# Moving the router products of the second stage from the head of a tile to behind the transposes of its activated rows

## The chip, the cores and the metric

The kernel runs on one NeuronCore of a Trainium2 chip. The metric is the device time of one execution in microseconds. Three runs of the kernel before are given, and one further execution was recorded by the hardware profiler; every duration used below is from that one.

## The reference, cut to what matters

The reference is one decoder layer over 2048 tokens (4 sequences of 512) with rows of 512 numbers. It has three blocks, each followed by a residual sum and a layer norm:

```python
x = _layernorm(x + attn(x, ...))       # 16 heads, chunked linear attention, gated group norm
x = _layernorm(x + xattn(x, token_ids, ctx, ctx, ctx))   # 4 experts, chosen by token id
x = _layernorm(x + ffn(x, gate_weight, gate_up, down))   # 48 kept experts, top 8 by a router
```

The second block is, for the one expert e to which a token belongs, with the same 512 by 512 matrix W three times:

```python
s = x @ W[e].T
y = (silu(s) * s) @ W[e]
```

The third block begins with a router, whose logits are taken from the rows that the second block has just normed:

```python
logits = x @ gate_weight.T              # 48 of the 128 columns are kept
top_v, top_i = top_k(softmax(logits), 8)
```

## The kernel before, in words

The kernel has three stages: attention (tiles of 128 tokens), the second block (called the second stage here), and the 48 experts with the closing norm. Each engine has its own list of instructions, written out by hand, and the engines meet through semaphores alone. An instruction that waits holds up everything behind it on its engine.

The second stage works on 19 tiles of 128 slots (`SLOT_T`), sorted by expert so that a tile has one expert. Every engine walks the tiles with `slot_tiles`, which calls its `b_tile(j, p, k, left, place)`: tiles 0 to 4 are written out, tiles 5 to 16 are a loop of three turns with four tiles in its body, and tiles 17 and 18 are written out again. Here j is the tile, p = j % 2 and k = j // 2; `is_later(j)` is true from tile 2 on.

Three tiles are in hand at once. TensorE's `b_tile(j)` (L898) issues, in this order:

- `route(p, k - 1)` (L890, matmuls at L895): the router's logits of tile j-2, four products of a 128x128 block of normed rows with 48 columns, which the profile shows as eight matmuls. It waits for ScalarE's copy of the transposed rows (`x2T_copied`) and ends in `lg_made`.
- `turn_h(p, k, 0)` (L875, L879): two transposes of the first half of `h1`, the activated rows of tile j. It waits for `h1_made`, which VectorE's `hidden` raises for each half (L1635).
- `expert_of(j)` (L853): TensorE's sequencer reads the number of tile j's expert from memory into a register (`value_load`).
- `turn_x` (L859, L863): four transposes of the gathered rows of tile j+1.
- `turn_h(p, k, 1)` (L879): two transposes of the second half of `h1`. It ends in `h1_turned`, on which ScalarE copies all of it, rounded, into `o_hi` (L1267).
- `turn_x2` (L883, L887): four transposes of the normed rows of tile j-1, for which it waits on `x2_made`.
- the down product of tile j: 12 matmuls at L629 of 512 columns (issued from L910), which wait for `o_high`, and from the ninth on for `h1_copied`.
- `up` of tile j+1: 24 matmuls at L629 of 256 columns. Each half raises `s_made`; ScalarE makes silu of it (L1253), VectorE multiplies (`hidden`, L1635) and raises `h1_made`.

VectorE's `b_tile(j)` has, in this order: `route(p, k - 1)` (L1637), which waits for `lg_made` of tile j-2 and is a chain of small instructions (L1642 to L1649); `low_h` (L1653), the rest of the activated rows that `o_hi` leaves over; `low_x1` (L1658), the same of tile j+1's gathered rows; `route_weights` (L1682 to L1699) of tile j-2; the residual sum of tile j at L1713, which waits for the down product (`y1_made`); its statistics (L1715, L1718); both halves of `hidden` of tile j+1 (L1635); and the norm of tile j (L1727), which ends in `x2_made`.

ScalarE's `b_tile(j)` has the copy to `o_hi` (L1267), the copy of tile j+1's gathered rows (L1246), one tanh for the router of tile j-2 (L1262), the copy of tile j-1's transposed rows (L1257), and the two silus of tile j+1 (L1253).

GpSimd's `b_tile(j)` has the gather of tile j+2's rows (an indirect DMA, L2095), two small instructions for the norm (L2124, L2126), and for tile j-2 the indirect DMAs of flags (L2116), normed rows with weights (L2102) and the seed of the output (L2109). SyncE's queue takes no part in the tiles of this stage.

The two banks that hold logits are guarded by `routed`, of which `route` wants the count of tile j-4.

Of the kernel before, what the change touches and what calls it, by code (L numbers as in the profile page):

```python
# [128 lines left out]
def build(nc, d):  # L129
    with ExitStack() as ctx:  # L130
# [306 lines left out]
        def at_least(eng, s, n):  # L437

            if not (isinstance(n, int) and n <= 0):
                eng.wait_ge(s, n)  # L440
# [5 lines left out]
        def is_later(n):  # L446

            return not (isinstance(n, int) and n < 2)

        def is_first(n):  # L450
            return isinstance(n, int) and n == 0
# [33 lines left out]
        def before_it(p, k):  # L485

            return 1 - p, k - (1 - p)

        def after_it(p, k):
            return 1 - p, k + p  # L490
# [131 lines left out]
        def _(pe):  # L622
            def three_passes(out, a_hi, a_lo, b_hi, b_lo, low=None, between=None):

                for i, (lhs, rhs) in enumerate(((a_hi, b_hi), (a_hi, b_lo), (a_lo, b_hi))):
                    if low and i == 2:
                        pe.wait_ge(*low)
                    for k in range(KC):
                        m = pe.matmul(out, lhs[:, k, :], rhs[:, k, :], start=(i == 0 and k == 0), stop=(i == 2 and k == KC - 1))  # L629
                        if between:  # L630
                            between(i * KC + k)
                return m
# [220 lines left out]
            def expert_of(j):  # L853
                return pe.value_load(eid_i[0:1, bass.ds(j, 1)], min_val=0, max_val=E1 - 1)

            def expert_part(w, e):
                return w[:, bass.ds(e, 1), :, :].rearrange("p a k n -> p (a k) n")

            def turn_x(p, k, place):  # L859
                pe.wait_ge(x1_got[p], 16 * (k + 1))  # L860
                at_least(pe, xg1_copied, 2 * k + p)
                for q in range(KC):
                    m = pe.transpose(ps[:, BT, q * P:(q + 1) * P], x1g[:, place, q * P:(q + 1) * P], eye[:, :])  # L863
                m.then_inc(xg1_turned, 1)

            def up(j, p, k):
                e = expert_of(j)
                pe.wait_ge(x_high, NT + 2 * k + p + 1)
                at_least(pe, h1_made, 2 * (2 * k + p))
                for half in range(2):  # L870
                    cols = slice(half * HALF_D, (half + 1) * HALF_D)
                    three_passes(ps[:, BS + half, 0:HALF_D], x_hi, x_lo, expert_part(w_hi, e)[:, :, cols], expert_part(w_lo, e)[:, :, cols],
                                 (xg1_copied, 2 * k + p + 1)).then_inc(s_made, 1)

            def turn_h(p, k, half):  # L875
                pe.wait_ge(h1_made, 2 * (2 * k + p) + half + 1)
                at_least(pe, h1_copied, 2 * k + p)
                for q in range(half * KC // 2, (half + 1) * KC // 2):
                    m = pe.transpose(ps[:, BH, q * P:(q + 1) * P], h1[:, q * P:(q + 1) * P], eye[:, :])  # L879
                if half:  # L880
                    m.then_inc(h1_turned, 1)

            def turn_x2(p, k, place):  # L883
                pe.wait_ge(x2_made, 2 * k + p + 1)
                at_least(pe, x2T_copied, 2 * k + p)
                for q in range(KC):
                    m = pe.transpose(ps[:, BX, q * P:(q + 1) * P], x2o[:, place, q * P:(q + 1) * P], eye[:, :])  # L887
                m.then_inc(x2_turned, 1)

            def route(p, k):  # L890

                pe.wait_ge(x2T_copied, 2 * k + p + 1)
                at_least(pe, routed, 2 * k + p - 1)
                for q in range(KC):
                    m = pe.matmul(ps[:, BL[p], 0:E2], x2T[:, q, :], router[:, q, :], start=(q == 0), stop=(q == KC - 1))  # L895
                m.then_inc(lg_made, 1)

            def b_tile(j, p, k, left, place):  # L898
                if is_later(j):
                    route(p, k - 1)  # L900
                turn_h(p, k, 0)
                e = expert_of(j)
                if left:
                    turn_x(*after_it(p, k), (place + 1) % 4)
                turn_h(p, k, 1)
                if not is_first(j):
                    turn_x2(*before_it(p, k), (place - 1) % 4)
                pe.wait_ge(o_high, NT + 2 * k + p + 1)
                at_least(pe, r2_made, 2 * k + p)
                three_passes(ps[:, BY, :], o_hi, o_lo, expert_part(w_hi, e), expert_part(w_lo, e),  # L910
                             (h1_copied, 2 * k + p + 1)).then_inc(y1_made, 1)
                if left:
                    up(j + 1, *after_it(p, k))
# [48 lines left out]
            add_rows(x1o[:, 1, :], hot_first[:, 1, :], last=True).then_inc(xg1_turned, 1)  # L962
            first_up()
            slot_tiles(pe, b_tile)
            route((SLOT_T - 2) % 2, (SLOT_T - 2) // 2)
            keep_warm(BH, 3)
# [1284 lines left out]
```

## Time and profile before

| what | value |
|---|---|
| median of 3 runs | 914.21 us |
| the three runs | 916.01, 913.24, 914.21 us |
| the profiled execution | 917.26 us |
| its span in the profile | 915.5 us |
| TensorE busy | 857.3 us, 94% |
| VectorE busy | 650.0 us, 71% |
| ScalarE busy | 402.2 us, 44% |
| GpSimd busy | 465.5 us, 51% |
| granted TensorE clock, mean | 0.987 of full speed |

The profiled execution stands 1.76 us above its own span and 3.05 us above the median of the runs. PE is TensorE, DVE is VectorE, ACT is ScalarE, POOL is GpSimd. A row of the timeline gives the start of a group of instructions in microseconds from the start of the span, how long it lasts, the engine, the line of the kernel, the operation with what it writes and reads, how many there are, and in brackets how long the engine sat idle before it and what ended that. The ends of matmuls are modelled, so starts are the safer numbers.

### The profile page before, as it was taken

Reading aid. Unit: us, or ns where it says so; the run is one execution under the profiler, and the core shown is the slowest. Engines: PE = TensorE matmul, PEld = TensorE weight load, DVE = VectorE, ACT = ScalarE, POOL = GpSimd, SP = SyncE. Lnnn points to the kernel's source line nnn. Section 1 sums busy time; section 2 is a strip of 40 time slices with the busy share of each in tenths; the row PEclk is TensorE's granted clock in tenths of the full one; section 3 lists DMA queues with packets and bytes.
Section 4 is the critical chain, followed back from the end, with each engine's and each line's share of the span. In section 5 each row is a group of like instructions: output and inputs, shape, how many; then the busy total and the mean of one; then the engine's idle time right before and its main releaser. Section 6 shows DMA issues by size and latency. Waiting matters only on the chain.

```text
span 915.5 us, 18727 instructions
## 1 busy us (share of the span) xinstructions
PE 857.3 (94%) x6020; PEld 722.9 (79%) x6021; DVE 650.0 (71%) x1475; ACT 402.2 (44%) x825; POOL 465.5 (51%) x441
## 2 busy tenths in 40 slices
PE   6899999999999978999999888999999999999985
PEld 4677777777777767888888677998998899888863
DVE  6856776567765774777777887767777677676876
ACT  4332333333333332332332145666666666666634
POOL 0332233433234241465555456776777777777454
PEclk9999999999999998999999899999999999999998
DMA  9461111211112017222322349999999999999975
GB/s 340 145 253 47 48 47 46 92 46 46 46 55 72 25 47 240 88 98 87 108 88 87 115 134 293 293 293 287 291 297 296 293 290 290 292 289 228 247 206 197
DMA packets 72430, 155.24 MB, mean 170 GB/s; under 512 B 9904, under 2 KB 10560, under 8 KB 72000
## 3 DMA queue, kind: packets, MB, share of 16 engines
q1 hardware_dynamic: 50240, 99.81, 33.7%
q0 software_dynamic: 22144, 54.85, 23.5%
q8 instruction: 25, 0.41, 0.2%
q14 instruction: 21, 0.17, 0.1%
HBM read 110.55 MB, written 44.07 MB: 169 GB/s over the span
## 4 chain that ended last, share of the span: by engine, by line
PE 68%; DVE 15%; issue 7%; ACT 4%; DMA 3%; POOL 1%; DVEq 0%; SPq 0%; ACTq 0%; POOLq 0%
PE ps L629 24%; PE ps L1029 18%; PE ps L1049 10%; PE ps L1018 3%; PE ps L734 2%; DVE arena L1514 2%; PE ps L724 2%; DVE arena L1453 1%; DMA xg<-x_rows,place_token 1%; DMA arena<-in_xT 1%; DVE arena L1447 1%; PE ps L810 1%; PE ps L895 1%; ACT o_hi L1267 1%; ACT arena L1119 1%
## 5 line engine op out<-in xcount | busy, mean ns | idle before, releaser
L2170 POOL DMA_INDIRECT y_rows<-arena,place_token x92 | 154.6, 1681 | 66.5 <-issue 48.3
L2159 POOL DMA_INDIRECT xg<-x_rows,place_token x96 | 94.4, 984 | 41.8 <-issue 27.1
L1029 PE MATMUL ps<-arena,raw 128*128 128x192 f32 x576 | 98.2, 327 | 1.4 <-DVE arena L1877 1.3
L1029 PEld LDWEIGHTS ps<-arena,raw 128*128 128x128 f32 x576 | 94.5, 190 | 4.8 <-issue 2.5
L629 PE MATMUL ps<-w_hi,x_hi 128*128 128x512 f32 (+1 forms) x324 | 76.1, 357 | 9.1 <-ACT arena L1119 4.7
L2025 POOL TENSOR_TENSOR arena<-arena,attn_pack 128x512 f32<-128x512 f32 x12 | 15.6, 1304 | 119.1 <-DVE arena L1465 119.1
L1029 PE MATMUL ps<-arena,mid_flat 128*128 128x192 f32 x432 | 73.2, 326 | 0.0
L629 PE MATMUL ps<-w_hi,x_lo 128*128 128x512 f32 (+1 forms) x324 | 73.2, 348 | 0.0
L1029 PEld LDWEIGHTS ps<-arena,mid_flat 128*128 128x128 f32 x432 | 71.0, 190 | 2.2 <-DVE arena L1877 0.3
L629 PE MATMUL ps<-w_lo,x_hi 128*128 128x512 f32 (+1 forms) x324 | 71.7, 343 | 0.0
L629 PEld LDWEIGHTS ps<-w_hi,x_hi 128*128 128x128 f32 x324 | 51.3, 189 | 21.1 <-issue 8.3
L1049 PE MATMUL ps<-down_parts,x_hi 128*96 128x512 f32 x192 | 62.8, 408 | 1.9 <-issue 1.9
L1479 DVE TENSOR_TENSOR arena<-ps,arena 128x512 f32<-128x512 f32 x16 | 11.1, 691 | 74.3 <-PE ps L681 60.3
L1049 PE MATMUL ps<-down_parts,o_hi 128*96 128x512 f32 x192 | 59.9, 393 | 0.0
L629 PEld LDWEIGHTS ps<-w_hi,x_lo 128*128 128x128 f32 x324 | 52.6, 190 | 9.3 <-issue 2.8
L629 PEld LDWEIGHTS ps<-w_lo,x_hi 128*128 128x128 f32 x324 | 53.7, 190 | 7.7
L2071 POOL TENSOR_TENSOR arena<-arena,minus_half 128x16 f32<-128x16 f32 x16 | 47.0, 2938 | 19.9 <-DVE arena L1471 19.9
L1253 ACT ACTIVATE arena<-ps 128x256 f32<-128x256 f32 x38 | 14.6, 384 | 86.6 <-PE ps L629 81.5
L629 PE MATMUL ps<-w_hi,o_hi 128*128 (+1 forms) x140 | 43.9, 425 | 7.1 <-ACT o_hi L1267 6.2
L1514 DVE TENSOR_TENSOR arena<-ps,arena 128x512 f32<-128x512 f32 x64 | 39.7, 683 | 14.0 <-PE ps L734 14.0
L1310 ACT ACTIVATE arena<-ps 128x192 f32<-128x192 f32 x48 | 15.8, 330 | 76.4 <-PE ps L1029 68.9
L1126 ACT ACTIVATE arena<-ps 128x512 f32<-128x512 f32 x32 | 18.9, 590 | 59.2 <-PE ps L629 55.1
(281 smaller groups left out, 2067.1 us busy)
## 6 DMA issues: line engine op xcount, KB each, us to landing
raw<-in_gu SPq DMA_DIRECT2D x24, 768.0 KB
mid_flat<-in_gu SPq DMA_DIRECT2D x18, 768.0 KB
raw<-in_dn SPq DMA_DIRECT2D x24, 256.0 KB
y_rows<-zero SPq DMA_DIRECT2D x20, 256.0 KB
mid_flat<-in_dn SPq DMA_DIRECT2D x18, 256.0 KB
arena<-in_gu SPq DMA_DIRECT2D x6, 768.0 KB
arena<-in_xT SPq DMA_DIRECT2D x16, 256.0 KB
x_res<-in_x SPq DMA_DIRECT2D x16, 256.0 KB, 2.8
```

The source lines that it names most:

```text
L629: m = pe.matmul(out, lhs[:, k, :], rhs[:, k, :], start=(i == 0 and k == 0), stop=(i == 2 and k == KC - 1))
L724: m = pe.matmul(ps[:, PM, g * P:(g + 1) * P], wg2[:, g * P:(g + 1) * P], g1[:, :], start=True, stop=True)
L734: m = pe.matmul(ps[:, PS + j, g * P:(g + 1) * P], kT[rows, g, :], qT[rows, g, :], start=True, stop=True)
L1018: m = pe.transpose(ps[:, CT + q // 2, o:o + HALF], xg[:, place, h, q * P:(q + 1) * P], eye[0:HALF, 0:HALF])
L1029: m = pe.matmul(out, wgu[slot][:, q, part * P:(part + 1) * P], xgT[:, p, q, :], start=(q == 0), stop=(q == KC - 1))
L1049: m = pe.matmul(ps[0:HALF, bank + h, :], lhs, rhs, start=(i == 0), stop=(i == len(parts) - 1))
L1126: act.activation(buf[:, :], ps[:, bank, :], ACT.Silu).then_inc(done, 1)
L1310: act.activation(g_a[:, :], ps[:, CG, 0:CAP], ACT.Silu).then_inc(g_made, 1)
L1514: dve.tensor_tensor(by_place(weighted)[:, j], ps[:, PS + j, :].rearrange("p (g t) -> p g t", g=G), by_place(decay)[:, j], ALU.mult).then_i ...
L2071: pool.tensor_tensor(rms_inv[:, :], ms_eps[:, :], minus_half[:, :], ALU.pow).then_inc(rms_made, 1)
L2159: pool.indirect_dma_start(out=xg[:, place, h, :], out_offset=None, in_=x2_d, in_offset=bass.IndirectOffsetOnAxis(ap=place_token[:, 2 * n + ...
L2170: pool.indirect_dma_start(out=y2_d if p and n < DUAL else y_d, out_offset=bass.IndirectOffsetOnAxis(ap=place_token[:, 2 * n + h:2 * n + h ...
```

## The change

In TensorE's `b_tile`, the router products of tile j-2 are no longer the first thing that a tile issues. They come after the second pair of transposes of `h1` and before the transposes of tile j-1's normed rows. Nothing is added or removed, no wait is changed, and no other engine's list is touched.

```diff
             def b_tile(j, p, k, left, place):
-                if is_later(j):
-                    route(p, k - 1)
                 turn_h(p, k, 0)
                 e = expert_of(j)
                 if left:
                     turn_x(*after_it(p, k), (place + 1) % 4)
                 turn_h(p, k, 1)
+                if is_later(j):
+                    route(p, k - 1)
                 if not is_first(j):
                     turn_x2(*before_it(p, k), (place - 1) % 4)
                 pe.wait_ge(o_high, NT + 2 * k + p + 1)
```

## Rows read from the trace of the kernel before

**Rows 1.** The page: busy time, share of the span, instructions.

```profile
PE 857.3 (94%) x6020; PEld 722.9 (79%) x6021; DVE 650.0 (71%) x1475; ACT 402.2 (44%) x825; POOL 465.5 (51%) x441
```

**Rows 2.** The chain that ended last, 440 to 480 us: start, us, what.

```profile
461.63 5.87 PE ps L629 x36
...
469.25 0.60 ACT o_hi L1267
```

**Rows 3.** The timeline of PE, from the router products to the next down product.

```profile
467.34 0.98 PE L895 MATMUL ps<-router,arena 128*128 128x48 f32 x8
468.40 0.60 PE L863 MATMUL ps<-attn_pack,arena 128*128 128x128 f32 x4
468.83 0.38 PE L879 MATMUL ps<-attn_pack,arena 128*128 128x128 f32 x2
...
469.99 0.50 PE L629 MATMUL ps<-w_hi,o_hi 128*128 x1 [0.19 <-ACT o_hi L1267]
```

**Rows 4.** The timeline of DVE and ACT in the same tile.

```profile
464.79 0.69 DVE L1713 TENSOR_TENSOR arena<-ps,arena 128x512 f32<-128x512 f32 x1
466.56 0.42 DVE L1635 TENSOR_TENSOR arena<-ps,arena 128x256 f32<-128x256 f32 x1
467.95 0.42 DVE L1635 TENSOR_TENSOR arena<-ps,arena 128x256 f32<-128x256 f32 x1 [0.96 <-ACT arena L1253]
...
469.01 0.19 DVE L1642 TENSOR_TENSOR arena<-ps,kept_bias 128x48 f32<-128x48 f32 x1
...
467.54 0.38 ACT L1253 ACTIVATE arena<-ps 128x256 f32<-128x256 f32 x1 [1.05 <-PE ps L629]
```

**Rows 5.** The timeline of DVE around tile 10: first and last router instruction.

```profile
434.39 0.19 DVE L1642 TENSOR_TENSOR arena<-ps,kept_bias 128x48 f32<-128x48 f32 x1
...
438.27 0.25 DVE L1699 TENSOR_SCALAR arena<-arena 128x48 f32<-128x48 f32 x1
```

**Rows 6.** The timeline where TensorE waited for VectorE's half: tiles 0 and 1.

```profile
345.11 0.44 PE L879 MATMUL ps<-attn_pack,arena 128*128 128x128 f32 x2 [1.28 <-DVE arena L1635]
345.88 1.08 PE L863 MATMUL ps<-attn_pack,arena 128*128 128x128 f32 x4 [0.34 <-issue]
...
356.57 0.42 DVE L1635 TENSOR_TENSOR arena<-ps,arena 128x256 f32<-128x256 f32 x1 [0.95 <-ACT arena L1253]
...
357.05 0.44 PE L879 MATMUL ps<-attn_pack,arena 128*128 128x128 f32 x2
```

**Rows 7.** The timeline of a slow cycle, tile 7 to tile 8.

```profile
408.98 1.18 PE L629 MATMUL ps<-w_hi,o_hi 128*128 x4 [0.34 <-ACT o_hi L1267]
411.15 1.00 POOL L2095 DMA_INDIRECT arena<-x_rows,slot_token  x1 [0.31 <-issue]
413.12 0.69 DVE L1713 TENSOR_TENSOR arena<-ps,arena 128x512 f32<-128x512 f32 x1 [0.97 <-PE ps L629]
414.88 0.84 DVE L1635 TENSOR_TENSOR arena<-ps,arena 128x256 f32<-128x256 f32 x2
416.38 0.66 PE L863 MATMUL ps<-attn_pack,arena 128*128 128x128 f32 x4 [0.47 <-DMA arena<-x_rows,slot_token]
...
418.03 0.72 PE L629 MATMUL ps<-w_hi,o_hi 128*128 x2 [0.34 <-ACT o_hi L1267]
```

**Rows 8.** The timeline of PE and ACT at the loop's turn, tile 12 to 13.

```profile
452.65 1.19 PE L629 MATMUL ps<-w_hi,o_hi 128*128 x4 [0.34 <-ACT o_hi L1267]
...
460.88 0.60 ACT L1267 ACTIVATE o_hi<-ps 128x512 fp32r<-128x512 f32 x1 [1.93 <-PE ps L879]
```

**Rows 9.** The timeline at the first and last down products that count.

```profile
366.63 0.73 PE L629 MATMUL ps<-w_hi,o_hi 128*128 x2 [0.34 <-ACT o_hi L1267]
...
495.62 0.73 PE L629 MATMUL ps<-w_hi,o_hi 128*128 x2 [0.31 <-issue]
...
503.63 1.19 PE L629 MATMUL ps<-w_hi,o_hi 128*128 x4
...
506.68 0.69 DVE L1713 TENSOR_TENSOR arena<-ps,arena 128x512 f32<-128x512 f32 x1 [0.20 <-PE ps L629]
```

## The prediction, made before the changed kernel was run

> **What bounds the kernel now.** I read the page first: TensorE is busy for 94% of the span, so what its queue does between two pieces of work counts [rows 1]. Then the chain of waits over the second stage, where every tile repeats one pattern. I call y(j) the first matmul of tile j's down product, and a cycle the time from y(j) to y(j+1). In cycle 13 the chain runs through the 36 matmuls of down and up product, through the router products and the transposes, and then leaves TensorE for ScalarE's copy to `o_hi` [rows 2]. So the head of a tile is a chain on two engines, and moving work in it can matter.
>
> The timeline gives the order from y(13) = 461.63: router products at +5.71, the four gathered-row transposes at +6.77, the second pair of `h1` (call its start t) at +7.20, the next down product at +8.36 [rows 2, 3]. Four transposes take 0.43 (468.40 to 468.83), so a pair takes 0.22, and the router products are the rest of the 1.06 between 467.34 and 468.40, which is 0.84. From t to the next down product there are 1.16: 0.42 until ScalarE starts, 0.60 of copy, 0.14 back. TensorE has only the x2 transposes to put there and sits idle for some 0.3.
>
> VectorE's rows in the same cycle: L1713 at +3.16, first `hidden` half at +4.93, second at +6.32, the router's first instruction at +7.38 [rows 4]. It is not on the chain today, but it is the engine that the logits go to.
>
> **The change, step by step.** All of it is in the 17 cycles from y(1) on. The cycles 2 to 16 take 495.62 - 366.63 = 128.99 us, 8.60 on average, and cycle 17 takes 8.01 [rows 9]. Nothing is added, no DMA and no other engine's list is moved.
>
> (a) The router products leave the head: -0.84 in front of the `h1` transposes. Not all comes back. The second pair needs the second `hidden` half: 467.95 + 0.42 + 0.06 from VectorE's end to TensorE's start (356.57 + 0.42 to 357.05 in rows 6) is y+6.80. So t moves from +7.20 to +6.80 at best, a gain of 0.40 [rows 4, 6].
>
> (b) Behind t now stand the pair (0.22), the router products (0.84) and the x2 transposes (0.43), 1.49, where ScalarE's copy asks for 1.16. The copy is hidden, and TensorE's own work is the longer by 0.33. (a) and (b) together: 6.80 + 1.49 = 8.29 for a cycle, 0.07 better than the 8.36 of cycle 13.
>
> (c) The logits get to VectorE later. The last router matmul ends 0.98 after the first starts [rows 3]; with 0.04 for the way there (my estimate, from the 0.06 of rows 6 the other way and matmul ends that are modelled) VectorE's chain starts at t + 0.22 + 0.98 + 0.04 = t+1.24, so 0.25 before the next down product. Now it starts 0.98 before (469.01 against 469.99 in rows 3, 4). Behind that wait stand, in order, `low_h`, `low_x1`, `route_weights`, L1713, the statistics and `hidden` of the next tile. From L1642 to the end of L1699 is 434.39 to 438.52, 4.13 [rows 5]. So L1713 comes at y - 0.25 + 4.13 = y+3.88, not at y+3.16. `low_h` is wanted only by the ninth matmul of the down product. Down and up product take about half each of the 5.87 [rows 2], so eight of the twelve take some 1.95: `low_h`, second in a chain of 4.13 that begins at y-0.25, has 2.2 for it, and the order of the list makes me count that as covered. The x2 transposes gain slack, since the norm they wait for is done before the router's chain begins.
>
> (d) L1713 to `hidden` is 1.77 (464.79 to 466.56), so the first half starts at y+5.65, ends at 6.07 and TensorE may start its first pair at 6.13, 0.42 after it has run dry at 5.71.
>
> (e) Between that pair and the gathered-row transposes the sequencer loads the expert's number. Where the pair itself had to wait for VectorE, those transposes came 0.77 after it (345.11 to 345.88), and not 0.22 [rows 6]. In cycle 7, with `hidden` at 414.88, they came 1.02 after the half was there (415.36 to 416.38) [rows 7]; the profile puts that wait down to the gather, and if that is right only the 0.77 stands. Today the router products cover this in most cycles: they are still executing while the sequencer passes the wait and loads. Moved away, they cover nothing. That gives y+6.90 for the transposes, t = 7.33 and a cycle of 7.33 + 1.49 = 8.82 at the least.
>
> The Trainium skill, TensorE: Matmul & The Clock Gate, "Architectural detail", gives TensorE a queue of 64 instructions. Taken as a rule, the sequencer would run ahead and the load cost nothing, (e) would fall away and the cycle be 8.29; rows 6 speak against it, with 0.77.
>
> (f) In cycle 7 L1713 came at +4.14 and not at +3.1, though VectorE was idle for 0.97 before it; it started 1.97 after a gather did (411.15) [rows 7]. Eight of the 17 cycles show such a delay, each with L1713 1.9 to 2.0 behind a gather's start. With L1713 due at 3.88 a gather between 1.9 and 2.9 would catch it, and one starts at +2.17 in cycle 7, whose cause (late statistics) becomes the rule. So L1713 lies between 3.88 and 4.14, and (e) between 0.77 and 1.02. Both high: 4.14 + 1.77 + 0.48 + 1.02 + 0.43 + 1.49 = 9.33.
>
> The Trainium skill, SBUF — State Buffer, "Who interferes with whom", says that a VectorE instruction with one SBUF input outside the two-port modes does not contend with GpSimd. L1713 has one; by that rule the lower 3.88 would stand. The trace shows the delay, so I don't rule it out.
>
> I take 4.0 and 0.85, since cycles of both kinds are about equally many: 4.0 + 1.77 + 0.48 + 0.85 + 0.43 + 1.49 = 9.0 us a cycle.
>
> (g) Where ScalarE turns its loop, the copy to `o_hi` starts only at 460.88, after 1.93 of idling and 8.23 after y(12), and the cycle is 461.63 - 452.65 = 8.98 whatever TensorE does [rows 8]. Cycles 8 and 12 have that. They neither gain nor lose at 9.0.
>
> (h) Cycle 17 has no gathered rows to turn, but the load and the late halves: 6.13 + 0.77 + 1.49 = 8.39, +0.4. After tile 18, L1713 came at 506.68, y+3.05, and the chain follows it to the next stage; at y+3.88 it is +0.8 [rows 9]. Cycle 1 changes by under 0.1.
>
> **Sum.** 15 x 9.0 = 135.0 against 129.0: +6.0; with +0.4 and +0.8: +7.2. Ends: 15 x 8.82 = 132.3, so +4.5; 15 x 9.33 = 140.0, so +12.2. The span would go from 915.5 to 922.7 and the profiled execution from 917.3 to 924.5. That execution stands 3.05 above the median of the runs; against the median the sum gives 914.2 + 7.2 = **921.4**, with ends 918.7 and 926.4. The expert stage waits for the end of this one, so the loss is passed on whole.
>
> **Rivals.**
> 1. *Not slower.* The expert's number is in the register before the pair is done, so (e) costs nothing. Then t is 6.80 even with the late first half (6.13 + 0.22 + 0.43 = 6.78), and the cycle is 8.29. Thirteen cycles of 8.29 and two of 8.98 are 125.7, -3.3; with +0.3 for cycle 17 and +0.8 at the end: -2.2, 912.0. For it: most cycles now show no gap there. Against it: in all of those the half was ready long before. It decides from the point where the load takes less than about 0.25.
> 2. *Half of it.* The logits or the load come sooner than I put them, by 0.2 to 0.3 a cycle, so that cycles are 8.65 to 8.8: +1.9 to +4.2, about 917. Both durations rest on few rows.
> 3. *Worse.* L1713 is caught by each gather and the load takes 1.02, or the gather itself arrives late: 9.33 or more, 926 and above. Cycle 7 is near that already, 418.03 - 408.98 = 9.05 with its router products in front [rows 7].
> 4. *Nothing.* The gain in (a) and the loss in (c) cancel, or the stage is covered by another. I see no cover: the chain stays on these lines for the whole stage.
>
> **How the numbers follow.** My forecast (cycles of 8.82 to 9.2) has 0.68, rival 1 0.13, rival 2 0.10, rival 3 0.07, rival 4 0.02. Some 0.3% (2.7 us) is what a measurement of this kernel can tell from no change. Slower by more is the forecast, rival 3 and most of rival 2: 0.82. Within it are rival 4, the rest of rival 2 and most of rival 1: 0.13. Faster by more is the rest of rival 1: 0.05. The range 915.5 to 925.5 holds the forecast, rival 2 and a little of rival 3.
>
> **What would show it.** Right: the router products at L895 start 0.2 after the second pair of L879; L1642 starts about 0.25 before the down product; L1713 at y+3.9 to 4.2; the first pair idles before it, released by L1635; the gathered transposes 0.75 to 1.0 after it; no idle time before the down product; most cycles near 9.0. Wrong: the gathered transposes right behind the first pair, cycles of 8.3, or L1713 still at y+3.1.

## The result and the profile after

The changed kernel took 919.15 us (median of 5 runs, 918.78 to 920.28) where the kernel before took 914.78 (5 runs, 913.24 to 916.01). The ratio is 1.0048, with an interval of 1.0031 to 1.0066. It is slower, by 4.4 us. The forecast was 921.4. Three single executions in the experiments below (two of the first one, one of the fourth) took 1420 to 2969 us, for no known reason, and stay out of all ratios.

TensorE does the same work in both kernels. The page of the kernel after, first its busy times (those of before are [rows 1]) and then the shares of the chain that ended last:

```profile
PE 857.4 (93%) x6020; PEld 722.2 (79%) x6021; DVE 648.6 (71%) x1475; ACT 404.1 (44%) x825; POOL 467.2 (51%) x441
PE 63%; DVE 22%; issue 8%; ACT 3%; DMA 2%; DVEq 0%; POOL 0%; SPq 0%; ACTq 0%; POOLq 0%
```

The same line of shares of the kernel before:

```profile
PE 68%; DVE 15%; issue 7%; ACT 4%; DMA 3%; POOL 1%; DVEq 0%; SPq 0%; ACTq 0%; POOLq 0%
```

No engine's busy time moved by more than 2 us. The chain has moved: 5 points of it went from TensorE, and 7 came to VectorE. The granted clock is 0.987 in both, so the clock has no part in the difference.

One cycle of the kernel after, from y(10) = 436.31 to y(11) = 445.23, in the timeline of all engines:

```profile
436.14 0.21 DVE L1642 TENSOR_TENSOR arena<-ps,kept_bias 128x48 f32<-128x48 f32 x1 [1.23 <-PE ps L895]
436.31 1.17 PE L629 MATMUL ps<-w_hi,o_hi 128*128 x4
...
438.29 0.98 POOL L2095 DMA_INDIRECT arena<-x_rows,slot_token  x1 [0.30 <-issue]
...
440.23 0.69 DVE L1713 TENSOR_TENSOR arena<-ps,arena 128x512 f32<-128x512 f32 x1
...
442.00 0.43 DVE L1635 TENSOR_TENSOR arena<-ps,arena 128x256 f32<-128x256 f32 x1
...
442.48 0.44 PE L879 MATMUL ps<-attn_pack,arena 128*128 128x128 f32 x2 [0.31 <-DVE arena L1635]
442.62 0.42 DVE L1635 TENSOR_TENSOR arena<-ps,arena 128x256 f32<-128x256 f32 x1 [0.20 <-ACT arena L1253]
...
443.32 0.65 PE L863 MATMUL ps<-attn_pack,arena 128*128 128x128 f32 x4 [0.40 <-issue]
...
443.81 0.38 PE L879 MATMUL ps<-attn_pack,arena 128*128 128x128 f32 x2
...
444.02 0.99 PE L895 MATMUL ps<-router,arena 128*128 128x48 f32 x8
...
445.05 0.21 DVE L1642 TENSOR_TENSOR arena<-ps,kept_bias 128x48 f32<-128x48 f32 x1 [1.27 <-PE ps L895]
...
445.23 0.95 PE L629 MATMUL ps<-w_hi,o_hi 128*128 x3
```

Read it from the top. The logits reach VectorE 0.17 before the down product (before: about 1.0 [rows 3, 4]). L1713 comes at y+3.92. The first half of `hidden` begins at y+5.69. TensorE's first pair starts at 442.48, y+6.17, released by L1635. The gathered-row transposes start 0.84 after the pair, and their row names no releaser but "issue". The router products then follow the second pair by 0.21, and nothing is idle before the next down product.

The chain of the kernel after, through the head of that tile (start, us, what):

```profile
442.00 0.44 DVE arena L1635
442.48 0.44 PE ps L879 x2
442.92 0.40 issue
443.32 0.65 PE ps L863 x4
443.97 0.22 PE ps L879 x2
444.19 0.84 PE ps L895 x8
445.05 0.22 DVE arena L1642
```

In the kernel before the chain goes through L629, the router products and the transposes and leaves TensorE for the copy at L1267 [rows 2]. Here the copy is off it. The chain comes from VectorE's `hidden`, passes the load and the router products, and goes back to VectorE's router chain. The two engines now wait for each other once in each tile.

The waits of the kernel after between 365 and 500 us say the same as totals (us in total, times, longest us):

```profile
DVE arena L1642 <- PE ps L895: 20.4, 16, 1.5
...
PEld ps L863 <- issue: 9.1, 15, 0.8
PEld ps L879 <- DVE arena L1635: 7.1, 15, 0.6
PE ps L863 <- issue: 5.8, 15, 0.5
```

Each of the three waits behind the first stands once in each of the 15 cycles. In the kernel before only four cycles (4, 7, 11 and 15) have a gap in front of L863; [rows 7] show one of them.

**The sum over the cycles.** From y(2) to y(17) the kernel after takes 498.45 - 365.60 = 132.85 us, 8.86 a cycle, against 128.99 [rows 9]: +3.86. Cycle 1 gave back 0.09, cycle 17 took 8.26 and not 8.01, +0.25. The end of the stage, in the timeline:

```profile
506.53 0.21 DVE L1642 TENSOR_TENSOR arena<-ps,kept_bias 128x48 f32<-128x48 f32 x1 [0.82 <-PE ps L895]
506.71 1.17 PE L629 MATMUL ps<-w_hi,o_hi 128*128 x4
...
510.00 0.68 DVE L1713 TENSOR_TENSOR arena<-ps,arena 128x512 f32<-128x512 f32 x1
```

L1713 of tile 18 comes at y+3.29 and not at y+3.05 [rows 9], +0.24. Together +4.26, close to the 4.4 of the medians. The two profiled spans differ only by 2.3. Ahead of the change, y(1) was already 0.94 earlier in the kernel after (357.32 against 358.26), and about another 1.0 is made up behind 510.00. Both lie outside what the change touches, and both move by more than that from one profiled execution to the next: y(1) stands at 351.82 in the first experiment below and at 357.31 in the one with L1713 late. So a single span can't be held against a median here, and the sum over the stage can.

### The profile page after: what moved, and what is told of

Same layout as the page of the kernel before. It is cut to its first block, busy times and chain, and to the rows that moved or that the text cites. A ratio compares the mean times of both kernels' runs of the same rounds, so it can differ in the third digit from the quotient of the medians.

```text
span 917.8 us, 18730 instructions
## 1 busy us (share of the span) xinstructions
PE 857.4 (93%) x6020; PEld 722.2 (79%) x6021; DVE 648.6 (71%) x1475; ACT 404.1 (44%) x825; POOL 467.2 (51%) x441
## 4 chain that ended last, share of the span: by engine, by line
PE 63%; DVE 22%; issue 8%; ACT 3%; DMA 2%; DVEq 0%; POOL 0%; SPq 0%; ACTq 0%; POOLq 0%
PE ps L1029 18%; PE ps L629 15%; PE ps L1049 11%; PE ps L1018 3%; PE ps L734 2%; DVE arena L1514 2%; PE ps L895 2%; PE ps L724 2%; DVE arena L1453 1%; DMA arena<-in_xT 1%; DVE arena L1447 1%; PE ps L879 1%; DVE arena L1715 1%; PE ps L863 1%; DVE arena L1713 1%
## 5 line engine op out<-in xcount | busy, mean ns | idle before, releaser
L629 PE MATMUL ps<-w_hi,x_hi 128*128 128x512 f32 (+1 forms) x324 | 76.1, 357 | 9.0 <-ACT arena L1119 4.7
L629 PE MATMUL ps<-w_hi,x_lo 128*128 128x512 f32 (+1 forms) x324 | 73.2, 348 | 0.0
L629 PE MATMUL ps<-w_lo,x_hi 128*128 128x512 f32 (+1 forms) x324 | 71.6, 343 | 0.0
L629 PEld LDWEIGHTS ps<-w_hi,x_hi 128*128 128x128 f32 x324 | 51.1, 189 | 21.4 <-issue 8.3
L629 PEld LDWEIGHTS ps<-w_hi,x_lo 128*128 128x128 f32 x324 | 52.6, 189 | 9.2 <-issue 2.8
L629 PEld LDWEIGHTS ps<-w_lo,x_hi 128*128 128x128 f32 x324 | 53.6, 189 | 7.7
L1514 DVE TENSOR_TENSOR arena<-ps,arena 128x512 f32<-128x512 f32 x64 | 39.7, 683 | 13.8 <-PE ps L734 13.8
L1299 ACT ACTIVATE arena<-ps,arena 96x512 f32<-96x512 f32 x46 | 31.5, 684 | 31.5 <-PE ps L1049 24.1
```

What stands on the lines that cost most here:

```text
L1299: act.activation(ye[:, p, 0, :], ps[0:HALF, CY, :], ACT.Copy, scale=w_col[:, p, 0:1]).then_inc(y_scaled[p], 1)
L1514: dve.tensor_tensor(by_place(weighted)[:, j], ps[:, PS + j, :].rearrange("p (g t) -> p g t", g=G), by_place(decay)[:, j], ALU.mult).then_i ...
```

## Experiments

All ratios are against the kernel before, run beside them on the same chip. "Cycles" are the 15 from y(2) to y(17) of the profiled execution, with a sum of 128.99 before and 132.85 after.

### The expert's number loaded first

In the changed kernel `expert_of` goes ahead of the wait for `h1`:

```diff
             def b_tile(j, p, k, left, place):
-                turn_h(p, k, 0)
                 e = expert_of(j)
+                turn_h(p, k, 0)
```

> The changed kernel with the load of the expert's number as the first thing of a tile's head, ahead of the first transposes. Theory (the change costs because the load stands uncovered behind a late first pair): the gathered-row transposes come 0.22 to 0.25 us after the first pair and not 0.75 to 1.0; L1713 stays at y+3.9, the first pair stays late at y+6.1; cycles of 8.3 us but for 8 and 12 (9.0); the kernel 7 us faster than the changed one, 912 us. Rival A (the gap in front of the gathered-row transposes is the gather or TensorE's own work, not the load): cycles stay at 8.85 us, 919 us. Rival B (the late first pair is the whole cost): the gap closes but the second pair is no earlier, 918 us or more.

Measured: 914.41 us, ratio 0.9996 [0.9976, 1.0015]. The whole loss is gone from the time, and 3.4 of the 3.86 us from the 15 cycles (129.45). The timeline of PE and DVE in cycle 3, y = 368.43:

```profile
374.61 0.44 PE L879 MATMUL ps<-attn_pack,arena 128*128 128x128 f32 x2 [0.33 <-DVE arena L1635]
...
374.89 0.60 PE L863 MATMUL ps<-attn_pack,arena 128*128 128x128 f32 x4
```

The gathered-row transposes now come 0.28 behind the first pair. TensorE still waits for VectorE's half, as it did after the change, but the next down product is at 376.75, 8.32 behind the last. That is the 8.29 of rival 1, in the first cycles. Later ones take up to 9.00, and cycle 7 (y = 402.28) shows why:

```profile
404.82 1.00 POOL L2095 DMA_INDIRECT arena<-x_rows,slot_token  x1 [0.30 <-issue]
...
406.02 0.25 DVE L1699 TENSOR_SCALAR arena<-arena 128x48 f32<-128x48 f32 x1
...
406.75 0.69 DVE L1713 TENSOR_TENSOR arena<-ps,arena 128x512 f32<-128x512 f32 x1 [0.48 <-PE ps L629]
...
408.99 0.44 PE L879 MATMUL ps<-attn_pack,arena 128*128 128x128 f32 x2 [0.70 <-DVE arena L1635]
```

L1713 could have started right behind L1699, at 406.2, and started at 406.75, 1.93 behind the gather. This is the hold of [rows 7], now at y+4.47. Eight of the 15 cycles have it, and the mean cycle is 8.63.

### The load first, with the router products where they were

```diff
             def b_tile(j, p, k, left, place):
+                e = expert_of(j)
                 if is_later(j):
                     route(p, k - 1)
                 turn_h(p, k, 0)
-                e = expert_of(j)
```

> The kernel before with the load ahead of the router products. Theory: only the cycles with a late first half (4, 7, 11, 15, a little 6, 10, 14) have the load uncovered; they fall from 8.8 to 9.05 to about 8.4 us, the others stay at 8.36; 2 us faster than before, 912.5 us. Rival A (those cycles wait for the gather): nothing moves, 914.8 us.

Measured: 912.54 us, ratio 0.9983 [0.9971, 0.9996]; the cycles sum to 126.72. Cycles 4, 7, 11 and 15 fell from 8.83, 9.05, 8.82 and 8.75 to 8.46, 8.46, 8.61 and 8.36. Cycle 7 (y = 404.33) is the one of [rows 7]:

```profile
406.94 1.00 POOL L2095 DMA_INDIRECT arena<-x_rows,slot_token  x1 [0.30 <-issue]
...
408.68 0.69 DVE L1713 TENSOR_TENSOR arena<-ps,arena 128x512 f32<-128x512 f32 x1 [1.01 <-PE ps L629]
...
410.92 0.44 PE L879 MATMUL ps<-attn_pack,arena 128*128 128x128 f32 x2
...
411.19 0.60 PE L863 MATMUL ps<-attn_pack,arena 128*128 128x128 f32 x4
```

The hold of L1713 is still there, and it is even later in the cycle. But L863 follows the pair by 0.27, though its rows came by a gather that started 4.25 earlier, where in [rows 7] it was 5.23. In cycles 4, 11 and 15 of the kernel before all sixteen landings that the gather reports were in by y+5.61, and L863 still came 0.81 to 1.03 behind the end of the first half, so there it was the load alone. Cycle 7 is mixed. Its gather had fifteen landings by y+5.41 and the last at y+7.36, 5.19 behind its start, and L863 came at y+7.40. So the profile was right to name the gather; without that landing the load, with 0.85 behind the half as in cycle 11, would have let L863 go some 0.2 sooner (my estimate). In the run here the same landing came at y+6.60 and held nothing. Of the 2.3 us by which the cycles are shorter, 0.5 is cycle 8 (8.99 to 8.45), where ScalarE's copy was not late this time.

This version is faster than the changed kernel. Against the kernel before it gains 1.6 us, and its interval ends just below 1.

### Half of the router products on each side

The load first, then two of the four products in front of the first pair and two behind the second:

```diff
             def b_tile(j, p, k, left, place):
-                turn_h(p, k, 0)
                 e = expert_of(j)
+                if is_later(j):
+                    route(p, k - 1, 0, KC // 2)
+                turn_h(p, k, 0)
...
                 if is_later(j):
-                    route(p, k - 1)
+                    route(p, k - 1, KC // 2, KC)
```

> The load first, then two of the four router products, then the first pair, the gathered rows, the second pair, the other two products, the x2 transposes. Theory: before the second pair TensorE has 0.42 + 0.22 + 0.43 us to do, just what the second hidden half takes (y+6.80), and behind it 0.22 + 0.42 + 0.43 = 1.07, under the 1.16 of ScalarE's copy, so a cycle is 6.80 + 1.16 = 7.96 us but for 8 and 12 (9.0); the logits start VectorE's chain at y-0.34, L1713 at y+3.8, the first half is there at y+6.05, in time behind the two products. 7 us faster than before, 907.5 us. Rival (VectorE's cycle is the bound once its chain starts late): cycles of 8.3 or more, 911 us or more.

Measured: 914.55 us, ratio 0.9983 [0.9965, 1.0]. Cycles 1 to 4 take 8.01 to 8.15. The timeline of PE at the end of cycle 3, y = 371.07:

```profile
376.79 0.54 PE L896 MATMUL ps<-router,arena 128*128 128x48 f32 x4
...
377.17 0.40 PE L879 MATMUL ps<-attn_pack,arena 128*128 128x128 f32 x2
...
378.16 0.54 PE L896 MATMUL ps<-router,arena 128*128 128x48 f32 x4
...
379.09 1.19 PE L629 MATMUL ps<-w_hi,o_hi 128*128 x4
```

With two products as cover the pair is at y+6.10 and no time is idle in front of it. From cycle 5 on L1713 comes at y+4.32 to 4.68 in all cycles but 8, 12 and 16, 1.8 to 2.1 behind a gather. Cycle 7 (y = 404.48) takes 9.32, and there the gathered rows themselves were late:

```profile
412.15 0.66 PE L863 MATMUL ps<-attn_pack,arena 128*128 128x128 f32 x4 [0.31 <-DMA arena<-x_rows,slot_token]
```

The last of the gather's sixteen landings is recorded at y+7.62, 4.81 behind its start, and L863 came at y+7.67. The sum is 127.56, and the cycles of 8.0 that were expected throughout lasted only as long as L1713 was not held.

### VectorE's router chain behind the rest of the activated rows

```diff
             def b_tile(j, p, k, left, place):
+                low_h(p, k)
                 if is_later(j):
                     route(p, k - 1)
-                low_h(p, k)
```

> The changed kernel with VectorE's router chain moved behind low_h, so that its wait for the logits holds up one instruction less. Theory (the wait for the logits at the head of VectorE's list makes it late): low_h starts at y-0.43 and L1713 comes at y+3.7 in place of 3.9; the first half and with it the cycle 0.2 us earlier, 8.65 us; 916.5 us. Rival (VectorE is late for its own work or by GpSimd's DMAs, not by this wait): L1713 stays at y+3.9, 919 us.

Measured: 919.19 us, ratio 1.005 [1.0032, 1.0069], the same as the changed kernel. L1713 came at y+3.69 to 3.71 in cycles 2, 4, 8, 12 and 16 and at up to y+3.95 in the others. The five cycles are 0.15 to 0.20 shorter than the same ones of the changed kernel, nearly as much as L1713 came sooner (0.18 to 0.20). So the place of L1713 does count. In the other ten the edit gave L1713 little, because TensorE's signal that the down product is done was itself recorded only at y+3.65 to 3.93 (see "Who holds L1713"). The mean cycle is 8.77 against 8.86, 1.3 us in all, of which 0.4 is lost again behind tile 18, where L1713 came at y+3.70 and not at y+3.29. The medians show nothing of the rest.

### The gather behind the norm: a misreading of mine

Three kernels were meant to take the gather out of L1713's way:

```diff
             def b_tile(j, p, k, left, place):
-                if left == 2:
-                    gather(j + 2, p, k + 1, (place + 2) % 4)
...
                 pool.tensor_tensor(rstd2[:, :], ve2[:, :], minus_half[:, 0:1], ALU.pow).then_inc(rstd_made, 1)
+                if left == 2:
+                    gather(j + 2, p, k + 1, (place + 2) % 4)
```

That edit in the kernel before:

> The kernel before with GpSimd's gather of the rows of tile j+2 moved from the end of its round (2 us or so before L1713) to right behind the two small instructions of the norm, at y+5.9. Theory (in eight cycles L1713 is held up to 1.9 to 2.0 us behind the start of a gather): no cycle has L1713 later than y+3.2; the cycles of 8.45 to 9.05 fall to 8.36 but for 8 and 12 with ScalarE's late copy; 2 us faster than before, 912 us. Rival (any indirect DMA of GpSimd holds it, so that the seed now does, or it is a place in the code): delays of 0.5 to 1.1 us stay in as many cycles, 914 us.

In the changed kernel with the load first:

> The changed kernel with the load first and the gather right behind the norm's two instructions. Theory: with neither the load nor the gather in the way every cycle is what the prediction summed for a load that costs nothing, 8.29 us, with L1713 at y+3.9; 15 cycles of 8.3 are 124.5 against 129.0 before, 910.5 us. Rival (it is VectorE's own chain that grows): L1713 at y+4.1 to 4.6 stays and so do cycles of 8.5 to 8.9, 914 us as with the load alone.

In the split kernel:

> The version with the load first and the router products in two halves, with the gather right behind the norm's two instructions. Theory: all cycles as its first ones were without the hold, 8.0 us; 15 of them 120.5 against 129.0 before; 906 us. Rival (holds of L1713 stay): cycles of 8.5 to 8.8, 914 us.

Measured: 1003.59 us, ratio 1.096 [1.0921, 1.0999]; 1006.18, 1.0983 [1.0942, 1.1023]; and 1004.27, 1.0966 [1.0924, 1.1009]. I had taken the rows to be wanted a cycle later than they are. They are gathered at y+2.2 and wanted at y+6.8. Behind the norm the gather is itself on the chain, in cycle 4 of the first of the three:

```profile
408.81 1.04 POOL L2095 DMA_INDIRECT arena<-x_rows,slot_token  x1 [0.24 <-issue]
...
412.34 1.11 PE L863 MATMUL ps<-attn_pack,arena 128*128 128x128 f32 x4 [2.69 <-DMA arena<-x_rows,slot_token]
```

The rows were used 3.5 us after the gather started, and the cycle is 13.66. The busy times by stretch of that kernel (stretch, length, then PE, PEld, DVE, ACT and POOL with their counts, granted clock, DMA share, GB/s) show a second price:

```profile
400.00:500.00 100.00, 80.87 (x406) 69.51 (x405) 49.30 (x165) 19.74 (x46) 33.66 (x43) 0.74 0.18 63
```

The granted clock was 0.74 of 2.4 GHz in the mean, so part of this stretch was run at 1.2 GHz, where TensorE sat idle for some 2.7 us in front of L863 in each tile. The three runs tell nothing about the hold.

### L1713 late, with the router products as cover

The kernel before with 0.7 us of idle work (statistics of a constant) on VectorE in front of L1713:

```diff
                     route_weights(p, k - 1, (place - 2) % 4)
+                    dve.bn_stats(filler[:, :], zero[:, :])
                 dve.wait_ge(y1_made, 2 * k + p + 1)
```

> The kernel before with one more instruction of VectorE, 0.7 us of statistics of a constant, between route_weights and L1713, so that L1713 comes at y+3.9 as in the changed kernel while the router products stay in the head. Theory (lateness of VectorE alone is covered by the router products; it costs only through the load, and less): the first pair stays at y+6.53, the gathered-row transposes at 6.9 to 7.1; cycles of 8.5 to 8.7, 915 us. Rival (the lateness is the whole cost, wherever the router products stand): cycles of 8.85 us, 918.5 us.

Measured: 917.72 us, ratio 1.0012 [0.9992, 1.0032]; the cycles sum to 130.13, +1.1. L1713 comes at y+4.03 to 4.23 in ten of the 15 cycles, later than in the changed kernel, and at y+3.59 to 3.70 in the other five. But the first pair stays at y+6.51 to 6.55, because the router products are still running. Cycle 6, y = 399.77:

```profile
405.47 0.99 PE L896 MATMUL ps<-router,arena 128*128 128x48 f32 x8
...
406.30 0.40 PE L880 MATMUL ps<-attn_pack,arena 128*128 128x128 f32 x2
...
407.08 0.65 PE L864 MATMUL ps<-attn_pack,arena 128*128 128x128 f32 x4 [0.38 <-issue]
```

Lateness under this cover costs some 30% of what the change costs in the cycles (1.1 of 3.86), and the median can't tell it from nothing. The last row shows where: in the worst cycles the half comes so late that the load shows again, with L863 0.78 behind the pair.

### Who holds L1713

The gather of tile j+3, taken from L2095's place to behind the norm's two instructions of tile j, so that it starts over a cycle sooner and the output's seed has its old place in the round:

```diff
-                if left == 2:
-                    gather(j + 2, p, k + 1, (place + 2) % 4)
...
+                if j + 3 < SLOT_T:
+                    gather(j + 3, 1 - p, k + 1 + p, (place + 3) % 4)
...
             gather(0, 0, 0, 0)
+            gather(2, 0, 1, 2)
```

In the kernel before:

> The kernel before with GpSimd's gather moved the other way: the rows of tile j+3 are gathered right behind the norm's two instructions of tile j, so at y+6, 9 us before they are wanted and some 5.5 us before the next L1713; the seed's DMA takes the gather's old place. Theory (a gather that starts 0.3 to 1.5 us before L1713 is due holds it): L1713 at y+3.05 to 3.2 in all cycles, cycles of 8.36 us but for the two at the loop's turn; 2 us faster than before. Rival (any indirect DMA in that place holds it, or it is no DMA at all): delays of 0.5 to 1.1 us in about as many cycles, the same time as before.

In the changed kernel with the load first:

> The changed kernel with the load first and this earlier gather. Theory: L1713 at y+3.9 and no later, cycles of 8.3 us, 4 us faster than before (with the load alone it was even with it). Rival: L1713 at y+4.4 to 4.6 and cycles of 8.5 to 8.9 as with the load alone, even with before.

In the split kernel:

> The load first, the router products in two halves, and this earlier gather. Theory: cycles of 8.0 us throughout, as the first ones were with the late gather; 15 cycles of 8.05 are 120.8 against 129.0, 8 us faster than before. Rival: L1713 at y+4.4 to 4.7, cycles of 8.5 to 8.8, 2 us faster or less.

Measured: 913.64 us, ratio 0.9986 [0.9969, 1.0004]; 917.31, 1.003 [1.0012, 1.0048]; 913.38, 0.9983 [0.9965, 1.0001]. The holds stayed in all three; L1713 came at up to y+4.15, 4.58 and 4.70, and the second kernel, expected 4 us under the kernel before, is above it. So a gather is not needed for a hold. In the third kernel the seed of the output stands where the gather was:

```profile
424.57 0.97 POOL L2113 DMA_INDIRECT y_rows<-arena,slot_token  x1 [0.30 <-issue]
426.56 0.69 DVE L1717 TENSOR_TENSOR arena<-ps,arena 128x512 f32<-128x512 f32 x1 [0.58 <-PE ps L629]
...
433.52 0.97 POOL L2113 DMA_INDIRECT y_rows<-arena,slot_token  x1 [0.30 <-issue]
...
435.34 0.69 DVE L1717 TENSOR_TENSOR arena<-ps,arena 128x512 f32<-128x512 f32 x1 [0.84 <-remote]
```

L1713 (here L1717) starts 1.99 and 1.82 behind it. The profile names TensorE once and "remote" once, but both are the same wait. The trace also records when semaphores are raised, and it has TensorE's raise of `y1_made`, which belongs to the last matmul of the down product, at y+4.32 and y+4.64 in these two cycles (9 and 10), 0.11 and 0.02 before L1713. By the profile that matmul ends at y+3.0, and TensorE's next matmuls start on time, at y+2.8. So VectorE is not held in its work: it waits for a signal of TensorE that comes late. The waits of the kernel before between 365 and 500 us say it too (us in total, times, longest us):

```profile
DVE arena L1713 <- PE ps L629: 6.0, 8, 1.0
```

In these eight cycles, among them that of [rows 7], the raise is recorded at y+3.53 to 4.15, 0.53 to 1.15 behind the end of its matmul, and L1713 starts 0.02 to 0.03 behind the raise. The raise comes 1.86 to 2.02 behind the start of the gather.

The last run takes one DMA out of the round. It is the changed kernel with the load first, without the seeds: the output is cleared with zeros in the first stage, and the residual rows are missing from it.

```diff
-                pool.indirect_dma_start(out=y_d, out_offset=bass.IndirectOffsetOnAxis(ap=slot_token[:, j:j + 1].bitcast(U32), axis=0),
-                                        in_=x2o[:, place, 0:D], in_offset=None).then_inc(y_seeded[p], 16)
+                pool.sem_inc(y_seeded[p], 16)
```

> The changed kernel with the load first and without the seeds: the normed rows are not scattered into the rows that the experts add to (those are cleared with zeros in the first stage), so the residual is missing from the output; GpSimd's round has one indirect DMA less. Theory (L1713 is held until some 2.0 us after the start of the last indirect DMA of GpSimd's round, gather or seed): the gather starts 1.3 us sooner, at y+1.3 in a cycle of 8.3 us, the hold would end at y+3.3, before L1713 is due at y+3.9; so L1713 at y+3.9 to 4.1 in all cycles, and cycles of 8.3 us where the load alone left 8.5 to 9.0. Some 5 us faster than the changed kernel with the load first in the second stage alone, and what the left out DMAs save at its end. Rival (a place in the code, or VectorE's own chain): L1713 at y+4.4 to 4.6 in the same eight or nine cycles, cycles of 8.7 to 8.9 us.

Measured: 912.58 us, ratio 0.9972 [0.9954, 0.9989]; the cycles sum to 126.17, 8.41 a cycle, where the load first alone gave 8.63. The gather is now the last DMA of the round and starts at y+1.09 to 1.60. Cycle 7, y = 406.39:

```profile
407.48 1.00 POOL L2097 DMA_INDIRECT arena<-x_rows,slot_token  x1 [0.30 <-issue]
410.30 0.69 DVE L1715 TENSOR_TENSOR arena<-ps,arena 128x512 f32<-128x512 f32 x1
```

L1713 (here L1715) starts at y+3.91, as its own list lets it, and no cycle has it later than y+4.14. TensorE's raise is on time in all 14 cycles that have a record of it, at y+2.99 to 3.08. Without the seed the late raises are gone. That is more than the theory said: by it a raise due 1.4 to 1.9 behind the gather, as here, would still have come late, as one due 1.42 behind it did in the kernel before (cycle 3, by 0.53). So the gather's earlier start alone doesn't explain it, and the runs don't tell what in GpSimd's round makes the raise late.

The changed kernel has the late raises too. In cycles 6, 7, 9, 10, 11, 13, 14 and 15 they are recorded at y+3.67 to 3.88, 1.85 to 1.92 behind the gather. They cost nothing there, since VectorE's own list isn't done before y+3.88. Nor is the rule of about 2 us complete. In cycles 3, 4, 8, 12 and 16 of the changed kernel, with the gather at y+2.28 to 2.36, L1713 started 1.5 to 1.6 behind it, so the raise had come before that. (In cycle 4 of the split kernel, where L1713 follows the gather by only 0.7, the raise at y+3.03 was as early as the gather itself.)

## Why the prediction was right, step by step

The direction, the mechanism of the loss and the range were right. The size was not: the sum over the stage gave +7.2 us, and the same rows of the two traces give +4.3, so 2.9 us were counted too much. (The predicted time missed by 2.3 only, since the median of before stands at 914.78 with two more runs.)

- (a), (b): right. The router products start 0.21 behind the second pair, and from the gathered-row transposes to the next down product there are 1.90 in the mean, against the 0.43 + 1.49 = 1.92 of the sum. No time is idle before the down product.
- (c): right. L1642 starts 0.09 to 0.18 before the down product, put at 0.25, and L1713 at y+3.89 to 3.99, put at 3.88 at best.
- (d): right. The first half starts at y+5.56 to 5.77 and the first pair at y+6.03 to 6.25, in the mean 6.14, where 6.13 was the low end.
- (e): right, and the larger part of the loss. The gathered-row transposes start 0.75 to 0.97 behind the pair in all 15 cycles, 0.82 in the mean, put at 0.85. Loading the number first took it away, and with it the loss (ratio 0.9996). The Trainium skill, TensorE: Matmul & The Clock Gate, "Architectural detail", has a queue of 64 instructions for TensorE; read as a promise that the load is free, it does not agree with the trace here, with 0.82 uncovered in each cycle. Of the 1.02 of rows 7, which the prediction took as the load's upper end, some 0.8 was the load; the rest was the gather's last landing, as the profile said.
- (f): the step that was mis-sized. I took L1713 at 4.0, half of the cycles held by a gather. None was: 3.91 in the mean, with gathers at y+1.80 to 2.36. And the mechanism was another: what comes late near GpSimd's DMAs is TensorE's raise of `y1_made`, which in eight cycles came at y+3.67 to 3.88, just before VectorE's own list was done. That none was held is luck: in cycles 6 and 15 the raise was 0.02 to 0.03 ahead of L1713. The Trainium skill, SBUF — State Buffer, "Who interferes with whom", would have given 3.88, which agrees with this kernel's trace. The later L1713 of the kernel that loads first, at up to y+4.6, is no case against it, since L1713 waited for the raise there. The first pair stood at y+6.14 in the mean where the sum had 4.0 + 1.77 + 0.48 = 6.25. With 0.11 for this, 0.03 for (e) and 0.02 for (b) the 9.02 of the sum becomes 8.86, the measured cycle. Against the rounded 9.0 that is 15 x 0.14 = 2.1 us of the miss.
- (g): the number right, the reason not, so this was luck. Cycles 8 and 12 took 9.01 and 9.02 against 8.98. But the copy to `o_hi` started at y+8.09 and 8.10, so with its 0.60 and the 0.14 back it was done at 8.84. What set these cycles was that L863 came 0.97 behind the pair, the most in the stage. Cycle 4 has the same 0.97, and all three lead into the first tile of a turn of the loop (5, 9 and 13). Why the load takes 0.2 more there is not shown.
- (h): half right. Cycle 17 took 8.26, put at 8.39. After tile 18 L1713 was late by 0.24, put at 0.8. That tile has no gathered rows to follow, so VectorE's chain has no `low_x1` in it, and from L1642 to L1713 it takes 510.00 - 506.53 = 3.47 and not 4.13. I had used a chain with an instruction that this tile doesn't have. These are 0.14 and 0.56, 0.7 us of the miss; cycle 1 has the last 0.09.

Rival 1 did not come true, but its cycle exists: 8.28 to 8.47 in cycles 2 to 5 once the load stands first. Later cycles are longer by the late raise. So the late half of (c) and (d) costs TensorE idle time that (a) pays back, as the prediction said, and what remained on the bill was (e).

## What to carry to other kernels

Work that stands in front of a wait may be there as cover: before it is moved, list every latency that runs under it, a register load in the sequencer among them, and not only the data it needs itself. Then look at what is queued behind the wait of whoever gets its result: here logits that nobody needed soon stood at the head of VectorE's list, and delayed the rows that TensorE needed next. A value that an engine loads from memory is best loaded ahead of that engine's next wait; this one line was worth all of the loss on the kernel after, and perhaps 0.17% on the one before (0.9983 [0.9971, 0.9996]).

## What the runs showed of the hardware

- The load of one number into TensorE's sequencer, behind a wait that has just been met, keeps the next matmuls back until 0.75 to 0.97 us after the pair in front; loaded ahead of the wait they follow by 0.27 to 0.31.
- An indirect gather of 128 rows could be used 3.5 us after its start (408.81 to 412.34). Its sixteen landings are mostly in after 3.2 to 3.6, but single ones came 5.19 (kernel before, cycle 7) and 4.81 us (split kernel, cycle 7) after the start, and TensorE waited for them.
- TensorE's raise of the semaphore of its down product was recorded up to 1.68 us behind the modelled end of the last matmul, and then 1.7 to 2.0 us behind the start of the last indirect DMA of GpSimd's round, in the kernels of the study and in most experiments. TensorE's next matmuls were not delayed. Without one DMA of the round (the seed) no raise was late. The cause is open.
- Where TensorE sat idle some 2.7 us in each tile of 13.4 to 13.8, its granted clock fell to 0.74 and 0.79 (400 to 500 and 500 to 600 us), against 0.987 over the whole span of both kernels of the study.
